# Six more filler products per image ahead of the mode sums, four behind them, and two waits of the fully connected loop in another order

## The chip, the cores and the metric

The kernel runs on one core of a Trainium2 chip. The metric is the time of one execution on the device in microseconds (us). TensorE appears in the profile as PE (products) and PEld (weight loads), VectorE as DVE, ScalarE as ACT, GpSimd as POOL, the DMA-issuing engine as SP.

## What is computed

32 images of 8 channels and 256 x 256 points go through two layers, each added to its input: a masked 3 x 3 convolution with a hidden width of 32, and a grouped Fourier operator of four layers. Cut to what matters here:

```python
x = x + _L0_conv_ref(_gn(x), ...)          # group norm, masked 3x3 convolution, relu, 1x1
# second layer, on _gn(x), 4 groups, 10 channels each:
h = _gconv1x1(h, fc0_w, fc0_b)
for i in range(4):
    h1 = _spectral_conv(h, sp_w1[i], sp_w2[i])   # rfft2, 24 x 12 modes mixed, irfft2
    h2 = _gconv1x1(h, w_w[i], w_b[i])
    h = h1 + h2
    if i < 3:
        h = _gswish(h, betas[i])
h = _gswish(_gconv1x1(h, fc1_w, fc1_b), betas[3])
return _gconv1x1(h, fc2_w, fc2_b)
```

## The kernel before

All matrix work is in float32. Each engine has its own program, written out by hand; semaphores with counted values order them. TensorE's program for one image is `image(i)`; four images are unrolled in a loop of eight turns. The order of the work is the order of the code. For one image TensorE does:

- the first convolution (lines 514, 524) and the first transform (545, 574);
- then, for each of the four layers, the **mode sums** (`summed`, line 590), which add up products that VectorE makes ten at a time (line 856; in layer 0 fewer, from the input's modes); **filler products** (`spin`, line 597), whose result nobody reads; the **inverse rows** (`inverse_rows`: line 619 in layers 0 and 2, line 615 in layers 1 and 3), which wait for VectorE to turn the sums into their operand `rot` (`mixed`, lines 1080 to 1095, short in layers 1 and 3, longer in 0 and 2); and the **pixel stage** (lines 697 and 707);
- after the pixel stage of layers 0 to 2 the forward transform, columns (636) and rows (655). VectorE scales its result (1128 to 1130) and makes the products (856) for which the next mode sums wait;
- the **fully connected loop**, 64 batches: batch m does two parts of fc1 (line 737), parts 2m and 2m+1, and then fc2 (line 748) for the two parts of the batch before. ScalarE applies SiLU to fc1's results (line 844, two activations a part); VectorE adds fc2's result to the residual (line 1179).

In the fully connected loop the second part of fc1 is behind two waits: `s_silu` says that ScalarE has read the banks of the part before, `s_fo` that VectorE has read the bank that fc2 of an earlier batch filled. A wait against a value that depends on the image is two things in TensorE's program: an instruction that computes the value into a register, and the wait itself, which sits on the instruction that follows it.

A filler multiplies a 128 x 128 table with 504 columns of another. A float32 product is two records in the trace, so three fillers are six.

Of the kernel before, what the change touches and what calls it, by code (L numbers as in the profile page):

```python
# [154 lines left out]
def program(nc, nb, x, conv1_w, conv1_b, conv2_w, conv2_b, lift_t, lift_b, lift_g, mix_w, mix_b, spec_w, betas,  # L155
            fc1_w, fc1_b, fc2_w, fc2_b, fwd_row, turn_id, fwd_col, inv_row, inv_col, grid, gridf, gmean, signs, out):
    with ExitStack() as ctx:
# [91 lines left out]
        HEAD_MM2, HEAD_X1, HEAD_OUT, HEAD_FO = 2, 2, 1, 2  # L249
        FFP = PU * BLOCKS - G  # L250
        STATS_AT = 55
        BATCHES = FFP // 2
# [39 lines left out]
        def group_of(a, n):  # L292
            return (a + 4 * n) // WID
# [17 lines left out]
        def fc_bank(p, r):  # L311

            return 4 * (p % 2) + r if r else 4 * (p % 4 in (1, 2))

        def sum_bank(m):

            return 7 if m == BATCHES else fc_bank(2 * m, 0)
# [167 lines left out]
        def _(pe):  # L485
# [10 lines left out]
            def group_sum(n, r, at):  # L496
                pe.wait_ge(s_stin, at + (r + 1))
                for layout in range(3):
                    mm = nc.tensor.matmul(gnps[n][:, 2 * layout + r:2 * layout + r + 1], gm[:, layout, :], mv[:, 3 * r:3 * r + 1],
                                          start=True, stop=True)  # L500
                mm.then_inc(s_stps, 1)
# [3 lines left out]
            def image(i):  # L505
# [74 lines left out]
                def summed(bank, g, pick, terms, first, last):  # L580

                    by = terms.rearrange("p (r o k s) -> p r o k s", r=2, o=WID, s=2)
                    for s in range(2):
                        begin, end = first and s == 0, last and s == 1
                        for t in range(2):
                            for back in range(2):
                                p = 64 * t + 32 * back
                                to = bass.AP(PS, 4096 * p + 512 * bank + 120 * g + KY * back,
                                             [[4096, 32], [-KY if back else KY, 2], [2 * KY, 5], [1, KY]])
                                mm = nc.tensor.matmul(to, sums[:, pick, :], by[:, :, t:WID:2, :, s], start=begin, stop=end,  # L590
                                                      tile_position=(0, p), skip_group_check=True)
                    return mm

                def spin(bank, count):

                    for _ in range(count):
                        nc.tensor.matmul(PS[:, bank, 0:504], gm[:, 0, :], rtab.rearrange("p a b c -> p (a b c)")[:, 0:504], start=True,
                                         stop=True)

                def inverse_rows(lay):  # L600

                    n = (i * 4 + lay) * 3
                    pe.wait_ge(s_ot, i * 4 + lay + 1)
                    pe.sem_inc(s_bank, 1)
                    for t in range(3):
                        bank, count = 4 * (t % 2), 4 if t < 2 else 2
                        if t == 2:
                            pe.wait_ge(s_gA, n + 1)
                            pe.wait_ge(s_gD, n + 1)
                            pe.sem_inc(s_bank, 1)  # L610
                        for g in range(G):
                            for a in range(count):
                                p, ch = 64 * (a % 2), 5 * g + 2 * t + a // 2
                                if lay % 2:
                                    mm = nc.tensor.matmul(PS[32 * g:32 * g + MODES, bank + a, 0:4 * NBLK * YY],  # L615
                                                          rot[p:p + 32 + KX, ch, 0, 0:MODES], invr[p:p + 32 + KX, :], start=True,
                                                          stop=True, tile_position=(p, 32 * g))
                                else:
                                    mm = nc.tensor.matmul(PS[:, bank + a, NBLK * YY * g:NBLK * YY * g + NBLK * YY],  # L619
                                                          rot[p:p + 32 + KX, ch, :, :].rearrange("p c m -> p (c m)"),  # L620
                                                          invr[p:p + 32 + KX, 0:NBLK * YY], start=True, stop=True,
                                                          tile_position=(p, 0), skip_group_check=True)
                        mm.then_inc(s_g, 1)
# [36 lines left out]
                def mode_sums(l):  # L660

                    done = i * PR + (SC + (l - 1) * WID)
                    for n in range(WID):
                        pe.wait_ge(s_pr, done + (n + 1))
                        for g in sorted({group_of(0, n), group_of(3, n)}):
                            strips = [a for a in range(4) if group_of(a, n) == g]
                            pick = 4 if len(strips) == 4 else 5 + strips[0] // 2
                            first = n == 0 or group_of(0, n - 1) < g and group_of(3, n - 1) < g
                            last = n == WID - 1 or group_of(0, n + 1) > g
                            mm = summed(1, g, pick, ring[n % 4], first, last)  # L670
                        mm.then_inc(s_sum, 1)
# [52 lines left out]
                    mm.then_inc(s_sum, 1)  # L724
                for lay in range(LAYERS):
                    if lay:
                        mode_sums(lay)
                    spin(2, 3 if lay % 2 == 0 else 1)
                    inverse_rows(lay)
                    pixels(lay)  # L730

                def fc1(p):

                    u, kg = divmod(p, BLOCKS)
                    k, g = divmod(kg, G)
                    for r in range(4):
                        mm = nc.tensor.matmul(PS[:, fc_bank(p, r), :], f1w[32 * r:32 * r + 31, k, g, :],  # L737
                                              hmem[32 * r:32 * r + 31, g * PART + u * ROW2:g * PART + u * ROW2 + ROW2],
                                              start=True, stop=True, tile_position=(32 * r, 0))
                        if r in (0, 3):  # L740
                            mm.then_inc(s_fc1, 1)

                def fc2(p, bank, first):

                    u, kg = divmod(p, BLOCKS)
                    k, g = divmod(kg, G)
                    for c in range(4):
                        mm = nc.tensor.matmul(PS[32 * c:32 * c + 32, bank, :], f2w[:, k, g, :],  # L748
                                              act(p)[:, c, :],
                                              start=first, stop=not first, tile_position=(0, 32 * c))  # L750
                    return mm
# [4 lines left out]
                for m in range(BATCHES + 1):  # L756
                    if m < BATCHES:
                        if m:
                            pe.wait_ge(s_silu, i * (2 * FFP) + (4 * m - 1))
                        if m == STATS_AT:  # L760
                            group_sum(0, 0, i * 4 + 4)
                            pe.wait_ge(s_stin, i * 4 + 6)
                        if m == STATS_AT + 1:
                            group_sum(0, 1, i * 4 + 4)
                            pe.wait_ge(s_var, i * 2 + 3)
                        fc1(2 * m)
                        if m:
                            pe.wait_ge(s_silu, i * (2 * FFP) + 4 * m)
                        if m > 1:
                            pe.wait_ge(s_fo, i * BATCHES + (m - 1 + HEAD_FO))  # L770
                        fc1(2 * m + 1)
                    if m:
                        pe.wait_ge(s_silu, i * (2 * FFP) + (4 * m + (m < BATCHES)))
                        fc2(2 * m - 2, sum_bank(m), True)
                        fc2(2 * m - 1, sum_bank(m), False).then_inc(s_fc2, 1)

            if nb >= TURNS:
                with pe.Fori(0, nb // TURNS) as j:
                    for k in range(TURNS):
                        image(j * TURNS + k)  # L780
            for k in range(nb - nb % TURNS, nb):
                image(k)
# [500 lines left out]
```

## Time and profile before

| what | value |
|---|---|
| median of 3 runs | 16871.61 us (16854.23 to 16873.06) |
| profiled execution, own time | 16896.35 us |
| its span (first to last instruction) | 16894.6 us |
| mean granted clock of TensorE in it | 0.979 of full speed |
| TensorE, VectorE, ScalarE busy | 95%, 44%, 64% |

One image takes some 523 us. The profile gives the granted clock of TensorE for any stretch: 1.00 is 2.4 GHz, 0.50 is 1.2 GHz, and a value between is a stretch with some of both. A product's end is modelled in the trace, and products overlap in it: two that follow each other without a gap show a start that lies before the other's end.

### The profile page before, as it was taken

To read this page: it belongs to the slowest core of one execution; us is meant where nothing else is said; L and a number is where in the kernel's file an instruction comes from. 1 tells how busy PE (TensorE), PEld (TensorE's weight loads), DVE (VectorE), ACT (ScalarE), POOL (GpSimd) and SP (SyncE) were. 2 spreads that over 40 slices of the span, in tenths; PEclk is the share of its full clock that TensorE was granted. 3 is DMA by queue.
4 is the path that set the end of the run, shared out by engine and by line. 5 is a ranking of instruction groups with operands and counts; after the bars stand their busy time and mean duration, and the time that the engine had idled before them with its cause. 6 is when DMAs were issued, how large, how long until landed. Compare 5 with 4: busy or idle time off the path is not lost.

```text
span 16894.6 us, 550984 instructions
## 1 busy us (share of the span) xinstructions
PE 15978.7 (95%) x240662; PEld 6755.8 (40%) x240662; DVE 7427.4 (44%) x9196; ACT 10807.5 (64%) x10372; POOL 66.5 (0%) x101
## 2 busy tenths in 40 slices
PE   4999999999999999999999999999999999999999
PEld 2344433344433444334444334443344433344333
DVE  4344543344434445434454334444344543345433
ACT  1765567755677655676556676557665567655667
POOL 0000000000000000000000000000000000000000
PEclk9999999999999999999999999999999999999999
DMA  1111111111111111111111111111111111111111
GB/s 45 43 34 43 39 40 43 34 46 39 38 46 38 40 39 42 39 46 34 43 39 40 43 37 43 38 42 40 43 37 42 38 40 44 34 43 38 40 43 35
DMA packets 512280, 679.95 MB, mean 40 GB/s; under 512 B 90930, under 2 KB 483338, under 8 KB 493718
## 3 DMA queue, kind: packets, MB, share of 16 engines
q1 hardware_dynamic: 507318, 642.77, 14.4%
q8 instruction: 1950, 31.95, 0.8%
q14 instruction: 604, 4.95, 0.1%
q10 hardware_dynamic: 2408, 0.28, 0.0%
HBM read 507.45 MB, written 135.27 MB: 38 GB/s over the span
## 4 chain that ended last, share of the span: by engine, by line
issue 76%; PE 22%; DVE 1%; ACT 0%; DVEq 0%; POOL 0%; DMA 0%; POOLq 0%; ACTq 0%; SPq 0%
PE PS L737 6%; PE PS L748 5%; PE PS L707 3%; PE PS L697 2%; PE PS L636 2%; PE PS L590 1%; PE PS L514 1%; PE PS L619 0%; PE PS L524 0%; PE PS L655 0%; ACT work L844 0%; PE PS L615 0%; POOL mv L1199 0%; DVEq L1120 0%; DVE work L1080 0%
## 5 line engine op out<-in xcount | busy, mean ns | idle before, releaser
L737 PE MATMUL PS<-hmem,fcw 31*128 31x512 f32 x32768 | 4479.7, 639 | 203.0 <-ACT work L844 57.3
L844 ACT ACTIVATE work<-PS 128x512 f32<-128x512 f32 (+1 forms) x4480 | 4231.5, 1028 | 477.8 <-PE PS L737 461.8
L737 PEld LDWEIGHTS PS<-hmem,fcw 31*128 31x128 f32 x32768 | 1301.3, 183 | 3321.2 <-ACT work L844 916.4
L837 ACT ACTIVATE hmem<-PS 128x2048 f32<-128x2048 f32 x1056 | 1983.1, 1878 | 758.6 <-PE PS L707 758.6
L1108 DVE STREAM_TRANSPOSE work<-hmem 128x2048 f32<-128x2048 f32 x864 | 1997.5, 2312 | 546.8 <-ACT hmem L837 502.9
L748 PE MATMUL PS<-work,fcw 128*32 128x512 f32 x17920 | 2192.8, 603 | 0.0
L1179 DVE SCALAR_TENSOR_TENSOR work<-PS,work 128x512 f32<-128x512 f32 x1056 | 730.7, 692 | 3143.1 <-PE PS L748 3143.1
L707 PEld LDWEIGHTS PS<-invc,gst 24*128 24x128 f32 x22528 | 1514.0, 330 | 1253.0 <-issue 1246.6
L844 ACT ACTIVATE gst<-PS 128x512 f32<-128x512 f32 (+1 forms) x2048 | 1994.0, 1037 | 1.5 <-PE PS L737 1.3
L707 PE MATMUL PS<-invc,gst 24*128 24x256 f32 x22528 | 1966.6, 463 | 1.6 <-issue 1.4
L816 ACT ACTIVATE gst<-PS 128x528 f32<-128x528 f32 (+1 forms) x384 | 201.0, 538 | 2634.4 <-PE PS L615 1601.0
L844 ACT ACTIVATE hmem<-PS 128x512 f32<-128x512 f32 (+1 forms) x1664 | 1613.1, 1021 | 141.6 <-PE PS L737 67.6
L1179 DVE SCALAR_TENSOR_TENSOR wspec<-PS,wspec 128x512 f32<-128x512 f32 x640 | 442.8, 692 | 1956.8 <-PE PS L748 1956.8
L697 PE MATMUL PS<-hmem,mix 30*32 30x512 f32 x33792 | 1236.8, 601 | 27.2 <-DVE gst L1102 21.4
L636 PE MATMUL PS<-work,fcol 32*24 32x512 f32 x30720 | 1168.8, 550 | 9.7 <-issue 9.0
L748 PEld LDWEIGHTS PS<-work,fcw 128*32 128x32 f32 x17920 | 460.4, 109 | 1566.0 <-issue 648.4
L748 PE MATMUL PS<-gst,fcw 128*32 128x512 f32 x8192 | 1066.2, 592 | 0.0
L590 PE MATMUL PS<-work,sums 128*32 128x120 f32 x22528 | 765.0, 295 | 192.9 <-DVE work L856 164.3
L748 PE MATMUL PS<-hmem,fcw 128*32 128x512 f32 x6656 | 886.4, 605 | 25.5 <-ACT gst L844 25.5
L824 ACT ACTIVATE hmem<-PS,c1b 128x1024 f32<-128x1024 f32 x256 | 285.3, 1114 | 855.8 <-PE PS L514 855.8
L514 PE MATMUL PS<-work,c1w 32*64 32x512 f32 (+1 forms) x12288 | 768.5, 610 | 29.9 <-issue 16.0
L590 PEld LDWEIGHTS PS<-work,sums 128*32 128x32 f32 x22528 | 680.0, 120 | 274.5 <-DVE work L856 232.8
(141 smaller groups left out, 10990.8 us busy)
## 6 DMA issues: line engine op xcount, KB each, us to landing
work<-in_x SPq DMA_DIRECT2D x1518, 128.0 KB, 2.5
wspec<-in_spec_w SPq DMA_DIRECT2D x768, 90.0 KB, 2.1
hmem<-x_d SPq DMA_DIRECT2D x128, 528.0 KB
x_d<-work SPq DMA_DIRECT2D x512, 128.0 KB, 2.9
wspec<-in_spec_w SPq DMA_DIRECT2D x768, 60.0 KB, 2.0
fcw<-fcw_d SPq DMA_DIRECT2D x32, 960.0 KB, 5.4
work<-x_d SPq DMA_DIRECT2D x384, 64.0 KB
wspec<-x_d SPq DMA_DIRECT2D x384, 64.0 KB
```

What stands on the lines that cost most here:

```text
L514: mm = nc.tensor.matmul(to[:, :, lo:hi], c1w[32 * r:32 * r + 32, dx, :], rows[32 * r:32 * r + 32, 2 * u:2 * u + 2, lo + dx - 1:hi + dx - 1 ...
L590: mm = nc.tensor.matmul(to, sums[:, pick, :], by[:, :, t:WID:2, :, s], start=begin, stop=end, tile_position=(0, p), skip_group_check=True)
L636: mm = nc.tensor.matmul(to, fcol[32 * r:32 * r + 32, b, :], part[32 * r:32 * r + 32, :, :, b, :], start=b == 0, stop=b == 7, tile_position ...
L697: nc.tensor.matmul(PS[32 * s:32 * s + 32, at + r, :], w, src, start=True, stop=True, tile_position=(32 * r, 32 * s))
L707: mm = nc.tensor.matmul(PS[:, at + r, y * W:y * W + W], gst[32 * r:32 * r + MODES, :, :, 2 * u + y].rearrange("p s o -> p (s o)"), invc[32 ...
L737: mm = nc.tensor.matmul(PS[:, fc_bank(p, r), :], f1w[32 * r:32 * r + 31, k, g, :], hmem[32 * r:32 * r + 31, g * PART + u * ROW2:g * PART + ...
L748: mm = nc.tensor.matmul(PS[32 * c:32 * c + 32, bank, :], f2w[:, k, g, :], act(p)[:, c, :], start=first, stop=not first, tile_position=(0, ...
L824: nc.scalar.activation(hid[u % 2][:, 0:1024], PS[:, bank:bank + 2, :].rearrange("p a b -> p (a b)"), ACT.Relu, bias=c1b[:, 0:1]).then_inc( ...
L837: nc.scalar.activation(unit(u), PS[:, at:at + 4, :], ACT.Silu).then_inc(s_hrow, 1)
L844: nc.scalar.activation(act(p)[:, strips, :], PS[:, bank:bank + (3 if rest else 1), :], ACT.Silu).then_inc(s_silu, 1)
L1108: V.transpose(to, unit(u)).then_inc(s_tr, 1)
L1179: V.scalar_tensor_tensor(rows, PS[:, sum_bank(m), :], f2b[:, 0:1] if nth == 0 else 0.0, rows, ALU.add, ALU.add).then_inc(s_fo, 1)
```

## The change

Two fillers are put ahead of the mode sums of layers 1, 2 and 3, into PSUM bank 3; behind the mode sums there are four fillers in place of three in layers 0 and 2, and two in place of one in layers 1 and 3. In the fully connected loop the wait for `s_fo` comes ahead of the wait for `s_silu`.

```diff
                 for lay in range(LAYERS):
                     if lay:
+                        spin(3, 2)
                         mode_sums(lay)
-                    spin(2, 3 if lay % 2 == 0 else 1)
+                    spin(2, 4 if lay % 2 == 0 else 2)
                     inverse_rows(lay)
                     pixels(lay)
...
                         fc1(2 * m)
+                        if m > 1:
+                            pe.wait_ge(s_fo, i * BATCHES + (m - 1 + HEAD_FO))
                         if m:
                             pe.wait_ge(s_silu, i * (2 * FFP) + 4 * m)
-                        if m > 1:
-                            pe.wait_ge(s_fo, i * BATCHES + (m - 1 + HEAD_FO))
                         fc1(2 * m + 1)
```

On TensorE, between the rows of the forward transform (L655) and the mode sums (L590) of layer 1; L664 computes the value of the wait for VectorE's products:

```order
 L655 MATMUL PS<-work,rtab 24x240 x3
 L655 MATMUL PS<-work,rtab 24x10x12 x8
+L597 MATMUL PS<-rtab,gm 128x504 x2
 L664 REGISTER_ALU
 L590 MATMUL PS<-work,sums 32x2x5x12 [waits products]
```

The two fillers stand behind the last row product and ahead of the wait.

On TensorE, between the mode sums and the inverse rows (L615) of layer 1; "modes_mixed" is VectorE's operand `rot`:

```order
 L590 MATMUL PS<-work,sums 32x2x5x12 [waits products]
 L590 MATMUL PS<-work,sums 32x2x5x12 x7
-L597 MATMUL PS<-rtab,gm 128x504
+L597 MATMUL PS<-rtab,gm 128x504 x2
 L603 REGISTER_ALU
 L615 MATMUL PS<-invr,work 24x264 [waits modes_mixed]
```

One filler more stands ahead of the same wait; layers 0, 2 and 3 have the same piece with their own counts.

On TensorE, one batch of the fully connected loop before; "silu_done" is `s_silu`, "result_ready" is `s_fo`, L768 and L770 compute the values of the two waits:

```order
L759 REGISTER_ALU
L737 MATMUL PS<-hmem,fcw 128x512 [waits silu_done]
L737 MATMUL PS<-hmem,fcw 128x512 x3
L768 REGISTER_ALU
L770 REGISTER_ALU [waits silu_done]
L737 MATMUL PS<-hmem,fcw 128x512 [waits result_ready]
L737 MATMUL PS<-hmem,fcw 128x512 x3
L773 REGISTER_ALU
L748 MATMUL PS<-work,fcw 32x512 [waits silu_done]
```

And now, where all lines of the loop are one further down:

```order
L760 REGISTER_ALU
L738 MATMUL PS<-hmem,fcw 128x512 [waits silu_done]
L738 MATMUL PS<-hmem,fcw 128x512 x3
L769 REGISTER_ALU
L771 REGISTER_ALU [waits result_ready]
L738 MATMUL PS<-hmem,fcw 128x512 [waits silu_done]
L738 MATMUL PS<-hmem,fcw 128x512 x3
L774 REGISTER_ALU
L749 MATMUL PS<-work,fcw 32x512 [waits silu_done]
```

The wait for ScalarE has moved from the second register instruction to the product itself; the wait for VectorE stands on the register instruction instead. No other engine's program changes.

## Rows read from the trace of the kernel before

**Rows 1.** The page: span, busy time of engines, granted clock in 40 slices.

```profile
span 16894.6 us, 550984 instructions
PE 15978.7 (95%) x240662; PEld 6755.8 (40%) x240662; DVE 7427.4 (44%) x9196; ACT 10807.5 (64%) x10372; POOL 66.5 (0%) x101
...
PEclk9999999999999999999999999999999999999999
```

**Rows 2.** The page: the chain of work that ended last, by engine.

```profile
issue 76%; PE 22%; DVE 1%; ACT 0%; DVEq 0%; POOL 0%; DMA 0%; POOLq 0%; ACTq 0%; SPq 0%
```

**Rows 3.** PE's waits: waited for, us in total, times, longest.

```profile
PE PS L590 <- DVE work L856: 164.3, 96, 1.7
```

**Rows 4.** Timeline of PE, layer 1: start, length, records, [idle before].

```profile
8151.73 1.02 PE L655 MATMUL PS<-work,rtab 96*24 96x240 f32 x24
8154.47 5.92 PE L590 MATMUL PS<-work,sums 128*32 128x120 f32 x192 [1.72 <-DVE work L856]
8160.32 1.11 PE L597 MATMUL PS<-rtab,gm 128*128 128x504 f32 x2
8161.58 2.83 PE L615 MATMUL PS<-invr,work 56*24 56x264 f32 x80
```

**Rows 5.** Windows, first mode sum to first filler, 96 stages: length, busy times, PEclk.

```profile
345.77:352.79 7.02, 7.01 (x192) 6.45 (x193) 5.34 (x9) 0.00 (x0) 0.00 (x0) 0.76 0.01 2
...
8154.47:8160.32 5.85, 5.85 (x192) 4.90 (x192) 5.06 (x9) 0.00 (x0) 0.00 (x0) 1.00 0.01 3
...
16583.52:16590.40 6.88, 6.88 (x193) 6.35 (x193) 5.24 (x9) 0.00 (x0) 0.00 (x0) 0.75 0.01 2
sum 620.64, PE 620.52 PEld 555.45 DVE 495.51 ACT 0.00 POOL 0.00; mean PE 6.46 PEld 5.79 DVE 5.16 ACT 0.00 POOL 0.00
```

**Rows 6.** Timeline, layer 2: the fillers, VectorE's last step, the inverse rows.

```profile
8214.20 2.80 PE L597 MATMUL PS<-rtab,gm 128*128 128x504 f32 x6
...
8216.84 0.72 DVE L1094 TENSOR_SCALAR work<-work,inside 128x960 f32<-128x960 f32 x1
...
8217.74 1.00 PE L619 MATMUL PS<-invr,work 56*128 56x66 f32 x14 [0.73 <-DVEq L1095]
```

**Rows 7.** Windows, layer 0, first inverse row to first column product, 32 images.

```profile
8106.41:8137.41 31.00, 30.80 (x609) 18.96 (x609) 22.99 (x13) 21.68 (x14) 0.00 (x0) 1.00 0.17 42
...
sum 1120.42, PE 1112.65 PEld 643.12 DVE 735.74 ACT 746.43 POOL 0.00; mean PE 34.77 PEld 20.10 DVE 22.99 ACT 23.33 POOL 0.00
```

**Rows 8.** Windows, layer 0, the first 4.2 us of that stage, two images.

```profile
4465.20:4469.40 4.20, 3.79 (x64) 3.65 (x64) 1.08 (x2) 4.20 (x3) 0.00 (x0) 1.00 0.53 132
...
7057.63:7061.83 4.20, 4.20 (x66) 4.20 (x66) 0.71 (x1) 0.97 (x2) 0.00 (x0) 0.86 0.44 107
```

**Rows 9.** Windows, the whole stage, the nine images whose clock falls early.

```profile
7057.63:7105.28 47.65, 47.65 (x608) 22.83 (x609) 22.98 (x13) 22.03 (x15) 0.00 (x0) 0.57 0.11 28
...
sum 361.41, PE 361.40 PEld 196.58 DVE 206.96 ACT 202.68 POOL 0.00; mean PE 40.16 PEld 21.84 DVE 23.00 ACT 22.52 POOL 0.00
```

**Rows 10.** Timeline of the fully connected loop, a pair of batches.

```profile
7901.45 2.08 PE L737 MATMUL PS<-hmem,fcw 31*128 31x512 f32 x16
...
7902.61 3.77 ACT L844 ACTIVATE work<-PS 128x512 f32<-128x512 f32 x4 [0.34 <-PE PS L737]
...
7905.32 2.33 PE L737 MATMUL PS<-hmem,fcw 31*128 31x512 f32 x16
7905.46 0.69 DVE L1179 SCALAR_TENSOR_TENSOR wspec<-PS,wspec 128x512 f32<-128x512 f32 x1 [3.17 <-PE PS L748]
...
7906.51 0.32 PEld L737 LDWEIGHTS PS<-hmem,fcw 31*128 31x128 f32 x8 [0.87 <-DVE wspec L1179]
...
7909.44 2.08 PE L737 MATMUL PS<-hmem,fcw 31*128 31x512 f32 x16
```

**Rows 11.** Timeline of the loop's end: the last activations and fc2.

```profile
8046.92 1.95 ACT L844 ACTIVATE gst<-PS 128x512 f32<-128x512 f32 x2
...
8048.92 1.07 PE L748 MATMUL PS<-hmem,fcw 128*32 128x512 f32 x8 [0.80 <-ACT gst L844]
```

## The prediction

> **What bounds the kernel now.** I read the page first. TensorE is busy 95% of the span and its clock stands at nine tenths or more in every slice [rows 1]; the chain that ended last is three quarters "issue" and most of the rest PE [rows 2], which means that TensorE runs its own program from end to end and hardly ever waits for something long. So the page hides what this change is about: short gaps, and what the clock does after them. For that I went to PE's waits, then to the timeline at the places of the diff, then to windows laid over one stage in all images. The reader is to see three things. First, ahead of the mode sums of layers 1 to 3 TensorE stands still 1.7 us each time, 96 times, 164 us in all [rows 3, 4]. Second, in many images the granted clock is at its lower level, 1.2 GHz, right behind such gaps, and the stage is longer there [rows 5, 7]. Third, in the fully connected loop the gap ahead of the second part of fc1 ends with the end of a ScalarE activation, though the view names VectorE [rows 10].
>
> **Part 1: two fillers ahead of the mode sums.** They start when the row products end, while VectorE scales and makes the first product of the stage. Their length: six records of three fillers take 2.80 us [rows 6], two records of one take 1.11 [rows 4], so a record more costs (2.80 - 1.11)/4 = 0.42 us, a filler 0.845, and two fillers 1.11 + 0.845 = 1.955 by modelled ends. The next product may start before that end: six steps of 0.42 are 2.54 of the 2.80, the other 0.26 is a slower first step and a tail, of which I take 0.16 as tail that the next product overlaps (an estimate), and the first filler starts a little before the modelled end of the product ahead of it, as the fillers of layer 1 do at 8160.32 against 8154.47 + 5.92 = 8160.39 [rows 4]. 1.955 - 0.16 - 0.07 = 1.72, against a gap of 1.72. The fillers just fill it. If the first mode sum came late by a tenth, it would cost nothing: the sums wait for VectorE's products one by one, VectorE being busy 5.06 of 5.85 us of the stage while at full clock TensorE has slack there [rows 5]. Cost: 0, at most 96 x (1.955 - 1.72 = 0.24) = 23 us if the modelled end had to be waited for.
>
> What it may give: of the 96 stages 55 show a mean clock between 0.75 and 0.76, the first and the last of which are shown, and take about 6.9 to 7.2 us; 41 are at 1.00 and take 5.85 [rows 5]. All together take 620.64 us; 96 x 5.84 would be 560.6. So the lower clock costs 60 us, and that is the price of its going away. Ahead of these stages TensorE did nothing for 1.7 us [rows 4]; with the gap filled I expect all 96 at 1.00. Bounds: 0 and 60; I take 60, because the only thing that sets these stages apart from the pixel stages is the gap.
>
> **Part 2: one filler more behind the mode sums.** In layers 0 and 2 three fillers end 0.73 us before the inverse rows start, since VectorE's last step of `mixed` ends late (8216.84 + 0.72 = 8217.56) [rows 6]. A fourth adds 0.845, less the 0.16 that may overlap: 0.69 of 0.73. Cost 0, at most 64 x 0.12 = 7 us. In layers 1 and 3 `mixed` is short: the one filler ends at 8160.32 + 1.11 = 8161.43 and the inverse rows start at 8161.58 [rows 4]. A second one ends its stream at 8161.43 + 0.845 - 0.16 = 8162.11, 0.53 us after the present start. Nothing covers that: ScalarE and VectorE wait for the inverse rows, and the pixel stage for them. Cost 64 x 0.53 to 64 x 0.70 (if the modelled end counts); I take 0.55, **35 us lost**.
>
> What the fourth filler may give is in layer 0. From the first inverse row to the first column product the stage takes 31.00 us at full clock; all 32 take 1120.42, 128 us more than 32 x 31.0 [rows 7]. Fifteen images carry that. I split them by the first 4.2 us of the stage: in nine the clock is down within it, as in the second row; in the other six it is still at 1.00 there, and they show a stall of 0.41 us inside the inverse rows instead, as in the first row (PE 3.79 of 4.20, ScalarE busy all the time) [rows 8]. The fourth filler closes the gap ahead of the inverse rows and so bears on the nine: 361.41 - 9 x 31.0 = 82 us [rows 9], the worst of them 47.65 us long. The six remain, since their stall lies behind. Bounds: 0 and 128; I take 82.
>
> On the cause, rows speak before any rule: 55 of 96 stages behind a 1.72 us gap have the low clock [rows 4, 5]. The Trainium skill, page "TensorE: Matmul & The Clock Gate", has two sections that disagree here. "Why this matters for your kernels" ties drops in mid-kernel to idle gaps longer than any of those filled here; by that the drops have another cause and the fillers give nothing, which is the second rival below. "A second HAM failure mode: psum-queue depth-cycling" has short idles between groups of products make the clock swing; by that the fillers give the 142 us above. The trace agrees with the second.
>
> **Part 3: the order of two waits.** Two batches repeat in 9.44 - 1.45 = 7.99 us [rows 10]. In the second of them the part of fc1 that starts at 7905.32 takes 2.33 us, in the first 2.08: the difference is a wait ahead of the weight load at 7906.51. VectorE was done at 7905.46 + 0.69 = 7906.15; ScalarE's four activations end at 7902.61 + 3.77 = 7906.38 [rows 10]. So `s_silu` comes last, 0.13 us before the load. Between the two stands, before, the register instruction for `s_fo`, which can't run ahead because the wait for `s_silu` sits on it. How fast is a load whose own wait ends last? At the loop's end: the activations end at 8046.92 + 1.95 = 8048.87, the product starts at 8048.92, 0.05 us later [rows 11]. Moving the register instruction out of the way gives 0.12 - 0.05 = 0.07 us. In the first batch of a pair the products flow (2.08), so neither order costs there, and with `s_fo` first a late VectorE would add about the same 0.07 where 0.25 of slack stand in the batch after it.
>
> Does 0.07 reach the end? The ring is: four activations, fc1's second part, fc2, fc1's first part of the next batch, and the four activations again, which had waited 0.34 us for PE [rows 10]. Every link is bound by the one before, so a pair gets 0.07 shorter, until ScalarE's 0.34 is used up. There are 31 such pairs in an image; around the statistics of the next image some three run differently. 28 x 32 x 0.07 = **63 us**. Bounds: 0, and 28 x 32 x 0.25 = 224 if all of the wait went.
>
> **The sum.** -60 - 82 + 35 - 63 = -170 us on the profiled execution's own 16896.35. That one is 24.7 above the median of 16871.61, and part of such a difference may be clock drops, so for the median I take 160: **16710 us**, 1% faster. I call 0.2% (34 us) what a measurement of this kernel can tell from no change.
>
> **Rivals.**
> - *The swap gives nothing.* If `s_fo` also comes late, the register instruction is only moved to the other wait. For it: the view names VectorE as releaser. Against: it is done 0.23 us earlier in the batch that matters. 16710 + 63 = 16773.
> - *The clock stays as it is.* The narrow products of these stages, not the gaps, bring it down; fillers then cost what they cost. For it: 41 stages of 96 have the same gap and full clock. 16871.6 - 63 + 35 = 16844, a change within 0.2%.
> - *Only layer 0 keeps its drops*, because the inverse rows bring them about, or the six become fifteen. For it: the six show that a stall inside the inverse rows does it as well [rows 8]. 16710 + 82 = 16792.
> - *Slower: the fillers hold up what follows them.* Its place is the handover from filler to wanted product: if each must wait for the filler's full end, 96 x 0.24 + 64 x 0.12 + 64 x 0.70 = 75 us are lost. It decides once the other gains together are under 40 us: with the clock unmoved and the swap worthless 16871.6 + 75 = 16947.
>
> **How the numbers follow.** The forecast 0.62, the swap worthless 0.12, layer 0 unchanged 0.08, the clock unmoved 0.12, slower 0.06. The first three are faster by over 0.2%, 0.82; the fourth is the same, 0.12. The range, 16640 to 16790, holds the first two and the third up to its middle: downwards 70 us for a swap worth up to double, upwards as far as the third. It leaves out the last two.
>
> **What the profile afterwards would show.** The wait of the mode sums for VectorE, 164 us, nearly gone; all 96 stages at clock 1.00 and 5.85 us; layer 0's stage at 31.0 us but for some six images; the stretch from the mode sums to the inverse rows of layers 1 and 3 longer by half a microsecond, with no idle ahead of the inverse rows; the pair of batches at 7.92 in place of 7.99, with the second weight load 0.05 us behind an activation's end. Wrong would be: low clock behind filled gaps, a pair still at 7.99, or idle time that has only moved behind the inverse rows.

## The result, and the profile after

The changed kernel takes 16707.34 us (median of 5 runs, 16646.96 to 16720.03) against 16854.23 us (5 runs, 16840.29 to 16873.06) of the kernel before on the same chip. The ratio is 0.9901 with a 95% interval of 0.9883 to 0.9919: faster by 1.0%.

The page of the changed kernel, to be read against [rows 1] and [rows 2]: span, the busy times, the chain that ended last.

```profile
span 16701.0 us, 552264 instructions
PE 16050.2 (96%) x241302; PEld 6720.8 (40%) x241302; DVE 7416.7 (44%) x9196; ACT 10807.2 (65%) x10372; POOL 66.3 (0%) x101
...
issue 97%; PE 3%; POOL 0%; DVE 0%; ACT 0%; POOLq 0%; DVEq 0%; ACTq 0%
```

The span is 193.6 us shorter. The medians differ by less, 16854.23 - 16707.34 = 147 us, since the profiled execution of before took 16896.35 us, 42 above the median. TensorE is *busier* by 71.5 us: it has 640 records more (ten fillers, 20 records, in each of 32 images) in a shorter time. Busy time does not say how the kernel does; the span and the stages do.

PE's waits after: waited for, us in total, times, longest.

```profile
PE PS L738 <- ACT work L845: 48.8, 62, 1.6
...
PE PS L697 <- issue: 26.8, 42, 4.1
...
PE PS L619 <- ACT gst L817: 1.2, 1, 1.2
```

The largest row of before, 164.3 us ahead of the mode sums [rows 3], is gone from the view, and so is the row of the inverse rows of layers 0 and 2 (L619 behind VectorE, 47.0 us before). A row to keep in mind is the second: waits of the pixel stage "<- issue", which means that no other engine was waited for. They were 8.9 us, 18 times, in the profile of before.

The same places in the timeline of the changed kernel as [rows 4], layer 1 of image 15, PE alone: start, length, records, idle before.

```profile
8059.53 1.01 PE L655 MATMUL PS<-work,rtab 96*24 96x240 f32 x24 [0.22 <-DVEq L1121]
8060.47 1.96 PE L597 MATMUL PS<-rtab,gm 128*128 128x504 f32 x4
8062.36 5.99 PE L590 MATMUL PS<-work,sums 128*32 128x120 f32 x192
8068.28 1.96 PE L597 MATMUL PS<-rtab,gm 128*128 128x504 f32 x4
8070.17 1.15 PE L615 MATMUL PS<-invr,work 56*24 56x264 f32 x32
```

Two fillers are 1.96 us (worked out beforehand: 1.955), they fill the gap, and no idle time stands ahead of the mode sums or of the inverse rows. Against the last row products the mode sums start at 8062.36 - 8059.53 = 2.83 us; in [rows 4] it is 8154.47 - 8151.73 = 2.74. The fillers hold the first sum up by 0.09 us.

The windows from the first mode sum to the first filler behind it, as in [rows 5]: window, length, busy times, granted clock, DMA share.

```profile
342.37:348.08 5.71, 5.71 (x193) 4.82 (x193) 4.95 (x9) 0.00 (x0) 0.00 (x0) 1.00 0.01 3
...
sum 550.78, PE 550.78 PEld 466.18 DVE 476.00 ACT 0.00 POOL 0.00; mean PE 5.74 PEld 4.86 DVE 4.96 ACT 0.00 POOL 0.00
```

All 96 stages are at 1.00; before, 54 were below it. (The prediction said 55 and counted one row too many.)

Layer 0 from the first inverse row to the first column product, as in [rows 7]: a usual image, the longest one, and the sum.

```profile
11607.14:11638.16 31.02, 30.82 (x609) 18.98 (x608) 22.99 (x13) 23.07 (x15) 0.00 (x0) 1.00 0.17 42
...
2353.12:2395.13 42.01, 40.84 (x610) 21.39 (x609) 22.99 (x13) 25.77 (x16) 0.00 (x0) 0.72 0.13 31
sum 1005.37, PE 997.79 PEld 611.10 DVE 735.54 ACT 750.66 POOL 0.00; mean PE 31.18 PEld 19.10 DVE 22.99 ACT 23.46 POOL 0.00
```

One image of 32 has a clock below 1.00 here, against fifteen before. Layer 2's inverse rows stood behind the same gap of 0.73 us and got the same fourth filler: its stage had two images below 1.00 before, and has none now. So the same gap goes with a fall less often there.

The timeline of the fully connected loop after, as in [rows 10]: a pair of batches, their activations and second weight loads.

```profile
7901.16 2.18 PE L738 MATMUL PS<-hmem,fcw 31*128 31x512 f32 x16
...
7902.32 3.77 ACT L845 ACTIVATE work<-PS 128x512 f32<-128x512 f32 x4 [0.17 <-PE PS L738]
...
7905.12 2.16 PE L738 MATMUL PS<-hmem,fcw 31*128 31x512 f32 x16
...
7906.14 0.31 PEld L738 LDWEIGHTS PS<-hmem,fcw 31*128 31x128 f32 x8 [0.71 <-ACT work L845]
7906.28 1.94 ACT L845 ACTIVATE hmem<-PS 128x512 f32<-128x512 f32 x2 [0.19 <-PE PS L738]
...
7909.07 2.18 PE L738 MATMUL PS<-hmem,fcw 31*128 31x512 f32 x16
```

The pair takes 7909.07 - 7901.16 = 7.91 us (7.99 before). The load at 7906.14 stands 0.05 us behind the end of the activations (7902.32 + 3.77 = 7906.09); before, it was 0.13. ScalarE's one gap of 0.34 us is now two, 0.17 and 0.19, so both batches are bound by the ring of ScalarE and TensorE, and the two parts of fc1 take nearly the same time (2.18 and 2.16 in place of 2.08 and 2.33).

The stages added up, in two profiles of each kernel (us; from windows laid over the stage in all images):

| stage | before | before again | changed | changed again | forecast |
|---|---|---|---|---|---|
| mode sums, layers 1 to 3 (96) | 620.64 | 605.85 | 550.78 | 550.71 | -60 |
| first filler to inverse rows, layers 1 and 3 (64) | 81.50 | 81.99 | 120.78 | 120.85 | +35 |
| layer 0, inverse rows to columns (32) | 1120.42 | 1098.22 | 1005.37 | 997.61 | -82 |
| layer 3, inverse rows to fc1 (32) | 1011.10 | 1032.51 | 1040.70 | 1059.65 | 0 |
| fully connected loop (32) | 8417.06 | 8437.25 | 8351.29 | 8341.76 | -63 |

The columns "again" are from experiments below. They matter: each profile is one execution, and the stages differ between two executions of one kernel by up to 22 us (layers 0 and 3 of before).

### The profile page after: what moved, and what is told of

The parts are those of the page before. It is cut to its first block, busy times and chain, and to the rows that moved or that the text cites. A ratio compares the mean times of both kernels' runs of the same rounds, so it can differ in the third digit from the quotient of the medians.

```text
span 16701.0 us, 552264 instructions
## 1 busy us (share of the span) xinstructions
PE 16050.2 (96%) x241302; PEld 6720.8 (40%) x241302; DVE 7416.7 (44%) x9196; ACT 10807.2 (65%) x10372; POOL 66.3 (0%) x101
## 4 chain that ended last, share of the span: by engine, by line
issue 97%; PE 3%; POOL 0%; DVE 0%; ACT 0%; POOLq 0%; DVEq 0%; ACTq 0%
PE PS L738 1%; PE PS L749 1%; PE PS L707 0%; PE PS L697 0%; PE PS L636 0%; POOL mv L1200 0%; PE PS L590 0%; PE PS L597 0%; POOL gst L1207 0%; PE PS L619 0%; ACT work L845 0%; PE PS L615 0%; DVEq L1121 0%; PE PS L655 0%; POOLq L1203 0%
## 5 line engine op out<-in xcount | busy, mean ns | idle before, releaser
L707 PE MATMUL PS<-invc,gst 24*128 24x256 f32 x22528 | 1928.1, 455 | 3.8 <-issue 3.8
L636 PEld LDWEIGHTS PS<-work,fcol 32*24 32x24 f32 x30720 | 639.2, 96 | 356.1 <-issue 135.2
L840 ACT ACTIVATE hmem<-PS 128x1024 f32<-128x1024 f32 x352 | 360.3, 1024 | 564.5 <-PE PS L707 564.5
```

Source lines behind the costliest of these rows:

```text
L636: mm = nc.tensor.matmul(to, fcol[32 * r:32 * r + 32, b, :], part[32 * r:32 * r + 32, :, :, b, :], start=b == 0, stop=b == 7, tile_position ...
L707: mm = nc.tensor.matmul(PS[:, at + r, y * W:y * W + W], gst[32 * r:32 * r + MODES, :, :, 2 * u + y].rearrange("p s o -> p (s o)"), invc[32 ...
L840: nc.scalar.activation(unit(u)[:, 0:2], PS[:, at:at + 2, :], ACT.Identity).then_inc(s_hrow, 1)
```

## The experiments

**Theory.** TensorE's clock falls behind short idle gaps; the fillers close them, and each of the three edits pays by itself. **Rivals:** the narrow products of these stages bring the clock down whatever stands ahead of them; the swap alone, or the fillers alone, does it all; the swap only moves the register instruction to another wait.

The kernel before, on the chip of the first four experiments, has a median of 16889.76 us, on that of the next four 16885.78, on that of the last three 16878.54; ratios are to these.

### Each edit alone

The swap alone:

```diff
                         fc1(2 * m)
+                        if m > 1:
+                            pe.wait_ge(s_fo, i * BATCHES + (m - 1 + HEAD_FO))
                         if m:
                             pe.wait_ge(s_silu, i * (2 * FFP) + 4 * m)
-                        if m > 1:
-                            pe.wait_ge(s_fo, i * BATCHES + (m - 1 + HEAD_FO))
```

> The kernel before with nothing but the two waits of the fully connected loop exchanged. My theory (the register instruction between the last wait and the weight load costs 0.07 us in 28 to 31 of 64 batches): 63 us less, a ratio of 0.996, with a pair of batches at 7.92 us in place of 7.99 and the clock drops of the mode sums as before. Rival (the swap is worth nothing, VectorE's wait only takes the other's place): ratio 1.000 and pairs at 7.99.

Measured 16825.38 us (6 runs, 16762.28 to 16838.06), ratio 0.9949 (0.9929 to 0.9968). Its timeline has the shorter pair, 8386.11 - 8378.20 = 7.91 us:

```profile
8378.20 2.18 PE L737 MATMUL PS<-hmem,fcw 31*128 31x512 f32 x16
...
8386.11 2.18 PE L737 MATMUL PS<-hmem,fcw 31*128 31x512 f32 x16
```

The whole loop takes 258.97 us in an image at full clock, against 261.01 before: 2.04 x 32 = 65 us. The mode sums still fall: 601.82 us, 38 of 96 below 1.00.

The fillers ahead of the mode sums alone:

```diff
                     if lay:
+                        spin(3, 2)
                         mode_sums(lay)
```

> The kernel before with nothing but the two fillers ahead of the mode sums of layers 1 to 3. My theory (the gap of 1.72 us brings the clock down): all 96 stages at 1.00 and 5.85 us, 60 us less, ratio 0.9965; layer 0's stage keeps its slow images. Rival (narrow products bring it down): about 55 of 96 stages low again, ratio 1.000.

Measured 16851.88 us (12 runs, 16794.19 to 16870.83), ratio 0.9976 (0.9964 to 0.9988): 0.24%, or 41 us. Its sum over the windows of the 96 stages:

```profile
sum 551.95, PE 551.65 PEld 465.07 DVE 476.32 ACT 0.00 POOL 0.00; mean PE 5.75 PEld 4.84 DVE 4.96 ACT 0.00 POOL 0.00
```

All 96 are at 1.00. The narrow products are the same as before, so they are not what brings the clock down. But layer 0, where nothing was changed, did not keep all of its slow images, though that had been expected. Its sum is

```profile
sum 1038.21, PE 1029.79 PEld 619.77 DVE 735.56 ACT 756.42 POOL 0.00; mean PE 32.18 PEld 19.37 DVE 22.99 ACT 23.64 POOL 0.00
```

Six images are below 1.00, two of them early, where the three other profiles with that gap (before, before again, the swap alone) have 1098.22 to 1120.42 with 15, 10 and 12, of which 9, 7 and 6 early. The profiled execution of this version is 29 us faster than its median, so it may be a lucky one.

The fillers behind the mode sums alone:

```diff
-                    spin(2, 3 if lay % 2 == 0 else 1)
+                    spin(2, 4 if lay % 2 == 0 else 2)
```

> The kernel before with nothing but one filler more behind the mode sums. My theory: layers 1 and 3 lose 0.55 to 0.6 us each time (35 to 39 us), layer 0's early drops go (82 us less), 45 us less in all, ratio 0.997; the drops of the mode sums remain. Rival (layer 0's drops come from the inverse rows themselves): ratio 1.002.

Measured 16836.12 us (10 runs, 16798.92 to 16871.48), ratio 0.9966 (0.9954 to 0.9978). Layer 0's stage, the sum over its 32 windows:

```profile
sum 1013.36, PE 1006.21 PEld 611.67 DVE 735.43 ACT 750.38 POOL 0.00; mean PE 31.44 PEld 19.11 DVE 22.98 ACT 23.45 POOL 0.00
```

No image falls within the first 4.2 us any more (nine before), two fall later. The mode sums, whose gap is left open here, still have 29 of 96 below 1.00 (18, 6 and 5 in layers 1, 2 and 3; 16, 16 and 22 in the first profile of before). In both experiments the falls right behind a filled gap are gone. Whether it also makes falls at other places rarer, as the 29 here and the six images above might suggest, or whether that is chance, no run separates. The three ratios multiplied give 0.9891, the whole change 0.9901: within the intervals the parts add up.

### The changed kernel without the filler that costs

```diff
-                    spin(2, 4 if lay % 2 == 0 else 2)
+                    spin(2, 4 if lay % 2 == 0 else 1)
```

> The changed kernel with one filler, as before, behind the mode sums of layers 1 and 3. My theory: that filler has no idle time to fill and no clock to hold, so the inverse rows of these layers start 0.6 us earlier, 64 times, and the kernel is 38 us faster than the changed one: ratio to the kernel before 0.988. Rival (the filler holds the clock for the inverse rows and the pixel stage behind it): drops appear in layers 1 and 3 and the time is that of the changed kernel or above, ratio 0.990 or more.

Measured 16703.54 us (5 runs, 16687.33 to 16723.41), ratio 0.9888 (0.9870 to 0.9906). The stretch to the inverse rows in layers 1 and 3 is back at 81.89 us from 120.78, 39 us less; the clock of the mode sums stays at 1.00 in all 96. These 39 us are 0.23% of the time; the two ratios differ by 0.13%, and their intervals do not resolve it. In the profile it is plain.

### The kernel before once more

No edit; a second profile of before, to see what of the first was chance.

> The kernel before once more, for a second profile. My theory: the waits for instructions in the last layer's pixel stage (5 us in the first profile of before, some 20 in that of the changed kernel) differ from one execution to the next and not by the change, so this one may show 20 or more as well; layer 0's early drops again in six to nine images. Rival (the change moved them there): 5 us again.

One run, 16898.83 us. The sum over its 96 windows of mode sums:

```profile
sum 605.85, PE 605.70 PEld 536.96 DVE 492.35 ACT 0.00 POOL 0.00; mean PE 6.31 PEld 5.59 DVE 5.13 ACT 0.00 POOL 0.00
```

42 stages are low in place of 54, and layer 0's stage takes 1098.22. How many stages fall varies from execution to execution of the same kernel. Seven images of layer 0 fall early (nine in the first profile). The waits "<- issue" of the pixel stage, which the expectation was about, are 21.6 us, 30 times, against 8.9 and 18 in the first profile: they differ between executions of one kernel, as was expected.

### Fillers of 8 columns ahead of the mode sums

The changed kernel, with the same number of products ahead of the mode sums, but short ones.

```diff
-                def spin(bank, count):
+                def spin(bank, count, cols=504):
...
-                        spin(3, 2)
+                        spin(3, 2, 8)
```

> The changed kernel, with 8 columns in place of 504 in the two fillers ahead of the mode sums: the same instructions in the same places, but TensorE stands still most of the 1.7 us again. My theory (the gap brings the clock down): about half of the 96 stages low again, 40 to 60 us more than the changed kernel, ratio to the kernel before 0.993. Rival (the added instructions move something else, such as the fetching of the program): all 96 stages at 1.00 and a ratio of 0.990.

Measured 16734.53 us (6 runs, 16700.97 to 16759.74), ratio 0.9918 (0.9899 to 0.9936). Layer 1 of image 15 in its timeline, and the sum over the 96 windows:

```profile
8061.43 0.61 PE L597 MATMUL PS<-rtab,gm 128*128 128x8 f32 x4
8063.23 6.91 PE L590 MATMUL PS<-work,sums 128*32 128x120 f32 x192 [1.18 <-DVE work L857]
...
sum 584.12, PE 583.99 PEld 499.84 DVE 490.27 ACT 0.00 POOL 0.00; mean PE 6.08 PEld 5.21 DVE 5.11 ACT 0.00 POOL 0.00
```

Of the gap 1.18 us are left, and 20 of 96 stages are low, against none behind a filled gap. That some product stands there is not enough; the time has to be filled. With the gap of 1.7 us the nearest version, the fillers behind alone, had 29, the others 38 to 54, so whether a shorter gap brings fewer falls is not settled. The mode sums take 33 us more than in the changed kernel, but the time, expected at 0.993, lies between that and the rival's 0.990, and its interval holds both.

### A counting instruction between the wait and the product

The changed kernel with the increment of a semaphore that no engine waits for, where the register instruction stood before: behind the wait for ScalarE, ahead of fc1.

```diff
                         if m:
                             pe.wait_ge(s_silu, i * (2 * FFP) + 4 * m)
+                        if m > 1:
+                            pe.sem_inc(s_bank, 1)
                         fc1(2 * m + 1)
```

> The changed kernel, with a semaphore count of TensorE's own put between the wait for ScalarE and the second part of fc1: the order of the waits stays as changed, but an instruction of the sequencer stands behind the last wait once more. My theory: the 0.06 to 0.07 us come back, a pair of batches takes 7.98 us again, some 55 to 60 us more than the changed kernel, ratio to the kernel before 0.993. Rival (what counted is which wait comes last): pairs at 7.92 us and a ratio of 0.990.

Measured 16857.26 us (12 runs, 16811.5 to 16890.72), ratio 0.9987 (0.9976 to 0.9999): the whole gain but for a tenth of a per cent is gone. Its timeline, a pair of batches:

```profile
8375.05 3.77 ACT L847 ACTIVATE work<-PS 128x512 f32<-128x512 f32 x4 [0.22 <-PE PS L738]
...
8377.90 2.21 PE L738 MATMUL PS<-hmem,fcw 31*128 31x512 f32 x16
...
8378.94 0.34 PEld L738 LDWEIGHTS PS<-hmem,fcw 31*128 31x128 f32 x8 [0.73 <-issue]
...
8385.94 2.21 PE L738 MATMUL PS<-hmem,fcw 31*128 31x512 f32 x16
```

The load stands 8378.94 - 8378.82 = 0.12 us behind the end of the activations, as it did before the change (0.13), and the pair takes 8.04 us. Over the image the loop at full clock goes from 258.97 to 262.42 us, 3.45 x 32 = 110 us: more than the swap had brought (65), since the first batch of a pair waits for ScalarE now too and pays as well. Expected were 55 to 60 us. The fillers are all there and the mode sums stay at 551.31. What stands between the last wait and the product it releases lies on the ring.

### One filler ahead of the fully connected loop

Ahead of the loop's first wait, on top of the kernel without the costly filler: wait for all but one of the same counts, then one filler.

```diff
+                pe.wait_ge(s_hrow, (i + 1) * (4 * PU) - 1)
+                pe.wait_ge(s_hlast, (i + 1) * PU - 1)
+                spin(0, 1)
                 pe.wait_ge(s_hrow, (i + 1) * (4 * PU))
                 pe.wait_ge(s_hlast, (i + 1) * PU)
```

> The version without the filler in layers 1 and 3, with one filler more ahead of the fully connected loop, where TensorE stands still 1.4 us in each image while ScalarE ends the last pixel row. My theory: a filler there ends before the wait does, so it costs nothing, and the images whose clock falls within the first 0.5 us of the loop go; 10 to 25 us less than that version, ratio to the kernel before 0.987. Rival (the drops at the loop's start come from the first batches' waits alone): ratio 0.9885, no change.

Measured 16673.83 us (5 runs, 16639.44 to 16687.67), ratio 0.9879 (0.9860 to 0.9899). PE's wait there falls from 45.4 us to the row shown, and the loop takes 8334.46 us against 8343.96, with 16 images below clock 1.00 in place of 23:

```profile
PE PS L738 <- DVE hmem L1174: 15.8, 32, 0.5
...
sum 8334.46, PE 8170.60 PEld 2195.95 DVE 1899.36 ACT 7761.88 POOL 27.48; mean PE 255.33 PEld 68.62 DVE 59.35 ACT 242.56 POOL 0.86
```

The direction is that of the theory at a fourth place; 10 us are too few for the times to show, and the interval holds the rival's 0.9885 as well.

### The changed kernel once more, and the second residual load later

The changed kernel itself, for a second profile of it.

> The changed kernel once more, on the same chip as the next two, to compare with: ratio to the kernel before 0.990, and no early drop in layer 0's stage.

Measured 16716.37 us (5 runs, 16712.29 to 16728.42), ratio 0.9910 (0.9897 to 0.9924), with no early fall in layer 0, as expected. Layer 3 from its inverse rows to fc1 takes 1059.65 us in it, 1040.70 in the first profile of the change, but 1011.10 in that of before. The trace shows where this is. In the longest such stages TensorE stands still in the middle of its own products, and no engine holds it up; timeline of the changed kernel, image 11, SP's queue and PE, and a window over the same place:

```profile
6123.52 0.35 SPq L446 DMA_DIRECT2D fcw<-fcw_d  x1
6123.91 4.22 SPq L433 DMA_DIRECT2D work<-x_d  x12
6128.18 4.03 SPq L433 DMA_DIRECT2D wspec<-x_d  x12
...
6132.15 1.08 PE L697 MATMUL PS<-hmem,mix 30*32 30x512 f32 x15
6137.37 1.96 PE L697 MATMUL PS<-hmem,mix 30*32 30x512 f32 x17 [4.14 <-issue]
...
6132.00:6140.00 8.00, 3.86 (x44) 1.10 (x44) 1.23 (x1) 1.02 (x1) 0.00 (x0) 0.79 0.51 110
```

Half of the DMA engines' time is taken in that window, with the loads that SP has issued since 6123.52: the weights of the fully connected loop, and both pieces of the residual. The trace also has the transfers that bring instructions (queue q8, kind "instruction", 16 KB each). Around this place one starts every 3.7 to 7.2 us; but none between 6121.42 and 6134.34, 12.9 us in which the loads run. That one lands at 6135.75, and TensorE goes on at 6137.37, 1.62 us later. In all 13 profiles together TensorE has 446 waits "<- issue" of 0.9 us or more, and each ended 1.2 to 1.8 us after such a transfer had landed, a condition that holds at 6% to 8% of evenly spaced moments. So these waits are waits for TensorE's own instructions.

Moving a load tests whether the loads hold the instructions up. The second piece was moved later, on the kernel without the costly filler:

```diff
                 residual(0)
-                residual(1)
                 for u in range(PU):
                     ...
                         load(following, n)
+                    if u == 0:
+                        residual(1)
```

> The version without the filler in layers 1 and 3, with the second piece of the residual loaded after the first unit of the fully connected loop in place of ahead of it. My theory (TensorE's waits for instructions in the last layer's pixel stage come of its program's fetches standing behind big loads): fewer and shorter such waits there, 44 waits of 0.9 us or more become some 36 (one an image is another wait), 10 to 30 us less than that version, ratio to the kernel before 0.987. Rival (the fetches are late for another reason): the same waits and a ratio of 0.989.

Measured 16647.72 us (4 runs, 16635.67 to 16658.5), ratio 0.9866 (0.9851 to 0.9881), 69 us under the changed kernel on the same chip; 39 of these are the filler left out. Layer 3's sum is 1021.46, against 1064.27 with the loads where they were (the kernel without the costly filler):

```profile
sum 1021.46, PE 950.16 PEld 525.39 DVE 487.14 ACT 409.25 POOL 0.00; mean PE 29.69 PEld 16.42 DVE 15.22 ACT 12.79 POOL 0.00
```

The waits "<- issue" of the pixel stage are 18.0 us (32 times) against 27.1 (37). Of those of 0.9 us or more inside layer 3's stage 5 are left of 13, as was expected. They are not gone, and one wait still takes 4.8 us. The time alone does not show the gain: the interval overlaps that of the kernel without the costly filler, 0.9870 to 0.9906.

### Both together

The last two experiments in one kernel.

> Both at once: the filler ahead of the fully connected loop and the later load of the residual's second piece, without the filler in layers 1 and 3. My theory: the two add up, ratio to the kernel before 0.985, the fastest of all. Rival (neither does anything): ratio 0.989.

Measured 16619.47 us (4 runs, 16602.83 to 16653.77), ratio 0.9856 (0.9840 to 0.9873), the lowest of all versions: 0.6% under the changed kernel on the same chip (16716.37). Layer 3's stage is at 1013.07 us with two waits for instructions of 0.9 us or more. The loop is at 8325.56 us with 10 images below clock 1.00, against 8341.73 and 21 in the version before it, which lacks the filler ahead of the loop.

## Why the prediction was right, and where its terms were off

The forecast was 16710 us, and the steps that carry it stood.

**The gaps set the clock: right.** In eight profiles with the gap ahead of the mode sums filled none of 96 stages is low; in the four with the whole gap 29 to 54 are, and 20 with fillers too short to fill it. With the fourth filler no image of layer 0 falls early in nine profiles; without it 9, 7, 6 and 2 do. The prediction's argument that only the gap sets these stages apart was too strong, since the same gap of 0.73 us went with a fall in 2 of 32 images in layer 2 and in 9 of 32 in layer 0; how often it does is not explained. "The clock stays as it is" is ruled out. The Trainium skill, page "TensorE: Matmul & The Clock Gate", section "A second HAM failure mode: psum-queue depth-cycling", has short idles between groups of products make the clock swing; the trace agrees, with 29 to 54 of 96 low stages behind a gap of 1.7 us and none behind a filled one.

**The term of the mode sums, -60: right for the profile it was taken from, too high for the kernel.** The stages fell from 620.64 to 550.78, 70 us, of which 96 x 0.09 to 0.10, some 9, are given back ahead of them, since the first sum starts 0.09 us later. The prediction had put this cost at nothing; the stage's slack takes it up, for it is that much shorter. But the other profiles with that gap (605.85 of before again, 601.82 of the swap alone, 593.29 of the fillers behind alone) make the term 33 to 45 by the same working (against 96 x 5.84 = 560.6), and the timing of the fillers ahead alone gives 41 us. That agreement is loose: in its profile layer 0 was 60 us or more shorter, and layer 3 36 us or more longer, than in the three without added fillers.

**The filler in layers 1 and 3, +35: 39 us.** The inverse rows start 120.78 / 64 - 81.50 / 64 = 0.61 us later, where 0.55 was taken from bounds of 0.53 and 0.70. It buys nothing that a run showed; leaving it out gives 39 us back.

**Layer 0, -82 and "the six remain": the first half right, the second failed.** The early falls went, all nine. Of the six late ones one was left in the first profile of the change, and the stage fell by 115 us. The step said that they would stay because their stall, inside the inverse rows, lies behind the filler. But the stall itself became rarer: the wait of the inverse rows for ScalarE was counted 6 times before and once in each profile of the change. Is that the filler's doing? In the other versions it was counted 3 to 5 times with the fourth filler, and 3, 6 and 5 times without it. Late falls were counted 1 to 4 times in the nine profiles with the fourth filler, and 6, 6, 4 and 3 times without it. The two overlap, and which images stall goes with how soon the inverse rows start: from layer 0's first mode sum it is 9.2 to 15.8 us in the first profile of before, and 9.2 to 9.95 in the six that stalled. That varies from execution to execution. Whether the filler did it stays open. The fourth filler's own cost, forecast at 0 to 7 us, was 4: the stretch from the first filler to the inverse rows grew from 112.9 to 116.4 us in layer 0 and from 113.5 to 114.5 in layer 2.

**The swap, -63: 65 us,** right in its mechanism too. The pair went from 7.99 to 7.91 (forecast 7.92; the prediction's own rows give 0.13 - 0.05 = 0.08 for the gain, where it wrote 0.07), the load stands 0.05 us behind the activations, and an instruction put back in that place takes the gain away and more. "The swap gives nothing" is ruled out by the swap alone, 0.9949.

**What the sum left out.** It came out at -170 on the first profile; the span fell by 193.6. By the stages it is -70 + 9 + 39 - 115 + 30 - 66 = -173; the other 20 us lie in stages that the table does not hold, 14 of them in layer 0's mode sums, which no edit touches. The +30 in layer 3 has no term in the prediction, and it may well be a cost of the change. Without added fillers the three profiles have 1011.10, 1032.51 and 1037.28 us there; the eight with added fillers and the loads in their place have 1038.53 to 1073.10, every one above; with the second load moved it is 1021.46 and 1013.07. Images with a wait for instructions of 0.9 us or more in this stage go the same way: 2, 5 and 6, then 7 to 14, then 5 and 2. That the fillers do it as further instructions to fetch is argued, not tested.

So two errors lie beside each other, layer 0 33 us too small and layer 3 not foreseen with 30, and the forecast is as close as it is partly by their cancelling. That 16707 lies 3 us from 16710 is luck as well: the time fell by 147 us here and by 162 on the chip of the last experiments, where 162 had been forecast (16871.61 to 16710).

## What to carry to other kernels

A mean clock near full speed (0.979 here) can hide a stage that runs far below it (0.57 in the longest of layer 0): lay windows over one stage in all its repetitions and compare their granted clock. Where short idle gaps stand ahead of the low ones, filling them with products nobody reads cost next to nothing here where the filler ended with the gap (4 us for the fourth filler), and its whole overhang where it did not (39 us), so each place needs its own count. Look at what the added instructions do elsewhere, too. Of several waits ahead of one instruction, let the one that ends last sit on that instruction, with nothing between.

## What the runs showed that was not expected

- One semaphore increment between the last wait and a product cost 3.45 us in each image, about 0.13 us in a pair of batches that takes 7.91; the register instruction in that place had cost 0.08.
- The kernel before, at the same gaps, had 54 low stages in one execution and 42 in another; behind the same gap a fall is a matter of chance, not a yes or no. So one profile over- or understates what a gap costs: 70 us by the first, 41 timed.
- In the changed kernel's pixel stage TensorE waited 4.14 us "<- issue" in the middle of its products, with loads filling half of the DMA engines' time, and the clock was at 0.50 right after it. It was waiting for its own instructions: their transfer started 12.9 us after the one before, and TensorE went on 1.6 us after it landed. That the loads held the transfer up is likely, not proven: moving one away took 43 us from the stage's sum, in one profile each, and left fewer such waits, but the times do not resolve what it brings.
